# Conv and attention hybrid: the softmax division moved to GpSimd, the row maximum written negated, the score scale put into the query weights

## The chip, the core and the metric

The kernel runs on one core of a Trainium2 chip. The core has five engines that run side by side and meet only at semaphores: TensorE (PE, matmuls and transposes, results go to PSUM), VectorE (DVE), ScalarE (ACT), GpSimd (POOL, which works on SBUF here) and SyncE (SP, which starts the DMAs). The metric is the device time of one execution in microseconds; lower is better.

## The reference

The input is four images of 16 x 16 positions with 192 channels. Two layers follow each other.

Layer 0 is a group norm, a convolution, four directional scans over 256 positions with 16 states for each of 96 channels, a norm, a gate, an output projection, and a residual. Layer 1 is, per image (256 tokens), a Performer attention with 12 heads, a residual, and then an attention in which only 6 of the 12 heads are kept, chosen by a router. The change lies in this last attention:

```python
logits = router_in @ Wr + br
_, top_idx = jax.lax.top_k(logits, K)            # K = 6 of 12 heads
...
q = proj(Wq, bq) * m                             # m keeps the chosen heads
k = proj(Wk, bk) * m
v = proj(Wv, bv) * m
scores = jnp.einsum('bhqd,bhkd->bhqk', q, k) / jnp.sqrt(jnp.float32(D))   # D = 16
probs = jax.nn.softmax(scores, axis=-1)
ctx = jnp.einsum('bhqk,bhkd->bhqd', probs, v)
```

Per image and chosen head the scores are 256 x 256, and the softmax runs along the last axis.

## The kernel before

Each engine has its own program, in the order in which its function issues instructions. The scans of layer 0 come first, as 96 slots (8 scans of 12 units). In a slot DVE runs one scan of 512 positions for 128 rows (line 965), GpSimd multiplies the states with c_rep (L542), and PE sums them (L1336). Other work of the layers is woven in beside the slots.

After the slots comes the list `rest`, made once by `side_work()`: pairs of a step's name and an image number. All engines walk this same list and issue what a step has for them. Images 0 and 1 overlap, then 1 and 2, then 2 and 3, so that two or three images are on their way at a time. The steps of an image's last attention are `wqk`, `wv` (weights of the chosen heads, by matmuls against a selection), `fq`, `fk`, `fv` (queries, keys, values), and then `s0 t0 s1 w0 t1 w1`, `fo` and `rn`. The step `s0` handles heads 0, 2 and 4, `s1` heads 1, 3 and 5; `t0`/`t1` and `w0`/`w1` go with them. In this text a **round** is three heads, so there are 8 rounds of 3 heads: 24 heads in all. What happens to a head in a round:

- `s`: PE writes the scores into one PSUM bank, [128, 2, 256] (query position, query half, key). DVE takes the maximum of each row from PSUM (`row_max`, L1068), waits for it, and makes the bias -max/4 in a second small instruction (L1073). ACT computes exp(score/4 + bias) for each query half into `prob` and adds the row up into `psum_row` (`exp_scores`, L727).
- `t`: DVE takes the reciprocal of the two sums (L1079), waits for it, and multiplies the two halves of `prob` by it (`divide_by_sum`, L1082). PE waits for both halves and transposes `prob` in 4 blocks (`turn_probs`, L1358). ACT copies the result from PSUM to `probT` (L590).
- `w`: PE multiplies the values with `probT` (`weigh_values`, L1369); DVE copies the sum (L1088).

Image parity p picks one of two sets of small buffers and of `prob`. In the trace the second set of `prob` and `probT` lies in a shared room and is named room_s; room_g holds `res` (among others), room_w the second `wsel`.

GpSimd has little in `rest`: one small power per norm (L486, the reciprocal root of the variance, for `yT`, `o`, `p`, `fo`), a gate product (`yn`, L556) and the last residual (`rn`, L559, 128 x 384). For `wqk`, ACT copies the weights of the chosen heads out of PSUM into `wsel`, in 6 copies (L590): four of them are for the queries, two for the keys.

## Time and profile before

| | us |
|---|---|
| median of 3 runs | 490.98 (490.72 to 491.32) |
| the profiled execution, own time | 493.81 |
| its span, first to last instruction | 491.9 |
| PE busy | 357.9 (73%) |
| DVE busy | 371.5 (76%) |
| ACT busy | 182.3 (37%) |
| POOL busy | 199.2 (41%) |
| mean granted TensorE clock | 0.889 |

A group row of the profile names a line, engine, operation and tiles with their shapes, the number of instructions, the time they were busy and the mean duration of one, and what the engine waited for before them. An idle gap costs nothing if the engine is not the one that the end waits for; the chain of waits tells which one that is. The granted clock is a share of 2.4 GHz.

### The profile page before, as it was taken

The page shows a single profiled execution, that of the slowest core. Times are in us where ns is not written, and L with a number is a line of the kernel's source. Part 1 is how long each engine was busy: PE and PEld are TensorE (multiplying, and loading weights), DVE is VectorE, ACT ScalarE, POOL GpSimd, SP SyncE. Part 2 cuts the span into 40 slices and gives each one's busy share as a digit, 9 for nine tenths or more (in the row PEclk, how much of TensorE's full clock was granted, in tenths as well). Part 3 has the DMA queues.
Part 4 walks back from the last instruction along what each step waited for, and adds up shares of the span by engine and source line. Part 5 has one row for each costly group of instructions (what it writes and reads, how often), then busy time and mean ns, then how long its engine had stood idle before and what let it go on. Part 6 is the DMA issues. An engine that isn't in the chain of part 4 may idle for free. (4 is left out here: it accounts for less than half of the span.)

```text
span 491.9 us, 5371 instructions
## 1 busy us (share of the span) xinstructions
PE 357.9 (73%) x1545; PEld 205.6 (42%) x1545; DVE 371.5 (76%) x712; ACT 182.3 (37%) x442; POOL 199.2 (41%) x199
## 2 busy tenths in 40 slices
PE   5530575669678785765999998994787999967652
PEld 4310121214223321221647545543665485956441
DVE  6264599999899999999988999987556637255562
ACT  2235354325555462342333332335224401125541
POOL 4406375756678585774554553450020001000001
PEclk9999979777999797996999999898598989596867
DMA  6402221110111112101101000000000000000000
GB/s 130 83 0 63 48 47 27 43 36 13 33 44 38 38 39 53 33 19 40 33 9 45 24 16 0 1 0 2 0 18 0 2 0 17 0 1 1 2 16 16
DMA packets 15741, 12.66 MB, mean 26 GB/s; under 512 B 7279, under 2 KB 11361, under 8 KB 15713
## 3 DMA queue, kind: packets, MB, share of 16 engines
q1 hardware_dynamic: 15713, 12.33, 10.9%
q8 instruction: 12, 0.20, 0.2%
q14 instruction: 16, 0.13, 0.1%
HBM read 2.62 MB, written 0.79 MB: 7 GB/s over the span
## 5 line engine op out<-in xcount | busy, mean ns | idle before, releaser
L542 POOL TENSOR_TENSOR outp<-state,c_rep 128x512 f32<-128x512 f32 x96 | 129.1, 1350 | 95.4 <-DVE state L965 47.9
L965 DVE TENSOR_TENSOR_SCAN state<-decay,inp_bc 128x512 f32<-128x512 f32 x96 | 117.2, 1221 | 6.7 <-DVE inp_bc L956 3.2
L1336 PE MATMUL y_acc<-outp,band 128*96 128x512 f32 x192 | 109.7, 657 | 6.7 <-DVE y_sum L980 3.2
L704 ACT ACTIVATE decay<-step_bc,a_neg 128x510 f32<-128x510 f32 x96 | 64.9, 684 | 55.5 <-PE step_bc L1323 55.3
L956 DVE TENSOR_TENSOR inp_bc<-b_rep,inp_bc 128x512 f32<-128x512 f32 x96 | 65.5, 682 | 9.9 <-PE inp_bc L1327 9.8
L1327 PE MATMUL inp_bc<-room_s,spread 96*128 96x512 bf16 x96 | 41.0, 427 | 42.8 <-DVE state L965 42.4
L486 POOL TENSOR_TENSOR rs<-mv,neg_half 128x2 f32<-128x2 f32 x16 | 11.2, 698 | 132.4 <-DVE mv L1001 132.4
L1323 PE MATMUL step_bc<-room_s,spread 96*128 96x512 bf16 x96 | 40.5, 422 | 17.4 <-DMA room_s<-lo 14.3
L1327 PEld LDWEIGHTS inp_bc<-room_s,spread 96*128 96x128 bf16 x96 | 9.8, 102 | 83.4 <-DVE state L965 79.3
L1336 PEld LDWEIGHTS y_acc<-outp,band 128*96 128x96 f32 x192 | 34.1, 182 | 23.0 <-issue 10.2
L1323 PEld LDWEIGHTS step_bc<-room_s,spread 96*128 96x128 bf16 x96 | 10.4, 108 | 37.7 <-issue 29.0
L692 ACT CAST hi<-step 96x512 bf16<-96x512 f32 x16 | 9.9, 616 | 35.8 <-DVE step L935 27.2
L1428 PE MATMUL ring<-kvw,tT 96*128 96x480 f32 (+1 forms) x48 | 22.1, 585 | 0.0
L532 POOL TENSOR_TENSOR lo<-step,mid 96x512 bf16<-96x512 f32 x16 | 19.4, 1232 | 3.4 <-ACT mid L696 3.4
L1422 PE MATMUL ring<-tT,qw 96*128 96x256 f32 (+1 forms) x64 | 15.3, 381 | 0.8 <-issue 0.8
L1313 PE MATMUL ring<-room_g,pre_w 96*128 96x512 f32 x16 | 10.1, 719 | 7.5 <-DVE room_g L890 7.5
L884 DVE SCALAR_TENSOR_TENSOR room_e<-room_w,cw,room_e 96x544 f32<-96x544 f32 x16 | 15.1, 947 | 0.5
L525 POOL TENSOR_SCALAR sps<-spe 96x512 f32<-96x512 f32 x8 | 4.9, 618 | 23.6 <-ACT spe L683 23.6
L696 ACT CAST mid<-step 96x512 bf16<-96x512 f32 x16 | 9.9, 616 | 12.3 <-DVE step L948 12.0
L1422 PEld LDWEIGHTS ring<-tT,qw 96*128 96x128 f32 (+1 forms) x64 | 11.9, 189 | 5.3 <-issue 4.0
L1428 PEld LDWEIGHTS ring<-kvw,tT 96*128 96x128 f32 (+1 forms) x48 | 9.2, 198 | 10.0 <-issue 10.0
L527 POOL TENSOR_TENSOR sps<-sps,spe 96x512 f32<-96x512 f32 x8 | 12.8, 1599 | 0.7
(392 smaller groups left out, 665.1 us busy)
## 6 DMA issues: line engine op xcount, KB each, us to landing
b_rep<-bc SPq DMA_DIRECT2D x64, 32.0 KB, 2.0
c_rep<-bc SPq DMA_DIRECT2D x64, 32.0 KB, 2.0
room_s<-hi SPq DMA_DIRECT2D x24, 64.0 KB, 2.0
room_s<-mid SPq DMA_DIRECT2D x24, 64.0 KB, 2.0
room_s<-lo SPq DMA_DIRECT2D x24, 64.0 KB, 2.0
x_tok<-in_x_dram SPq DMA_DIRECT2D x2, 384.0 KB, 3.8
out_dram<-room_g SPq DMA_DIRECT2D x4, 192.0 KB, 2.0
room_a<-in_L_attn_w_qkv_dram SPq DMA_DIRECT2D x1, 432.0 KB, 6.4
```

The lines of the kernel that those rows point to most:

```text
L527: g.tensor_tensor(sps[:], sps[:], spe[:], ALU.mult).then_inc(S["sp_s"], 1)
L532: g.tensor_tensor(lo[:, i, :], step2[:, i, :], mid[:, i, :], ALU.subtract).then_inc(S["lo"], 1)
L542: g.tensor_tensor(outp[:, u % SLOTS, :], state[:, u % STATE_SLOTS, :], c_rep[:, n % 2, :], ALU.mult).then_inc(S["outp"], 1)
L704: a.activation(decay[:, u % SLOTS, :, 1:L], step_bc[u % 2][:, :].rearrange("p (b l) -> p b l", b=IMG)[:, :, 1:L], ACT.Exp, scale=a_neg[:, ...
L884: v.scalar_tensor_tensor(sums, window, cw[:, i:i + 1], sums, ALU.mult, ALU.add).then_inc(S["conv"], 1)
L956: v.tensor_tensor(inp_bc[u % 2][:, :], b_rep[:, n % 2, :], inp_bc[u % 2][:, :], ALU.mult).then_inc(S["drive"], 1)
L965: v.tensor_tensor_scan(state[:, u % STATE_SLOTS, :], decay[:, u % SLOTS, :, :].rearrange("p b l -> p (b l)"), inp_bc[u % 2][:, :], 0.0, AL ...
L1323: t_.matmul(step_bc[u % 2][:, :], spread[:, q, :], stack[:, n % 2, j, 0:TOK], start=True, stop=True).then_inc(S["bc_step"], 1)
L1327: t_.matmul(inp_bc[u % 2][:, :], spread[:, q, :], stack[:, n % 2, j, TOK:2 * TOK], start=True, stop=True).then_inc(S["bc_inp"], 1)
L1336: t_.matmul(y_acc[0:DI, :], band[:, at:at + DI], outp[:, u % SLOTS, :], start=(g12 == 0), stop=(g12 == UNITS - 1)).then_inc(S["y_mm"], 1)
L1422: ins = t_.matmul(b_[:, u * L:(u + 1) * L], qw[0:CK + c, c, i * P:(i + 1) * P], tT[0:CK + c, c, at0:at0 + L], start=(c == 0), stop=(c == 1))
L1428: ins = t_.matmul(b_[:, 0:w], tT[0:CK + c, c, at:at + P], kvw[0:CK + c, c, j, :], start=(c == 0), stop=(c == 1))
```

## The change

Three edits belong together. (1) The row maximum is written negated by the reduction itself, and the second small instruction (L1073), its buffer and its semaphore go. (2) The factor 1/4 leaves the exponential and is applied where ACT copies the selected query weights out of PSUM: four of the six copies become an activation (Copy) with a scale. (3) DVE keeps the reciprocal, and the two products by it move to GpSimd, into the same steps `t0` and `t1` of its list. DVE's reciprocal gets a wait for the division that last used its buffer.

```diff
--- before.py
+++ after.py
@@ -332,7 +332,6 @@
         col = sb("col", [CK, 3, 2, IMG])
         hot = sb("hot", [CK, 2, 2, IMG, TOPK])
         nmax = [sb(f"nmax{i}", [P, PER_ROUND, 2]) for i in range(2)]
-        nmaxs = [sb(f"nmaxs{i}", [P, PER_ROUND, 2]) for i in range(2)]
         psum_row = [sb(f"psum_row{i}", [P, PER_ROUND, 2]) for i in range(2)]
         prec = [sb(f"prec{i}", [P, PER_ROUND, 2]) for i in range(2)]
 
@@ -349,7 +348,7 @@
         S["outd"] = [sem(f"s_outd{b}") for b in range(IMG)]
         S["x"] = [sem(f"s_x{h}") for h in range(HALVES)]
 
-        for n in ("key", "prob_max", "prob_bias", "prob", "prob_rec", "prob_divided", "weighed"):
+        for n in ("key", "prob_max", "prob", "prob_rec", "prob_divided", "weighed"):
             S[n] = [sem(f"s_{n}{i}") for i in range(2)]
         free = [sem(f"s_free{i}") for i in range(FINAL_RING)]
         beside, rest = side_work()
@@ -542,6 +541,14 @@
                 g.tensor_tensor(outp[:, u % SLOTS, :], state[:, u % STATE_SLOTS, :], c_rep[:, n % 2, :],
                                 ALU.mult).then_inc(S["outp"], 1)
 
+            def divide_by_sum(n, j):
+                p = n % IMG
+                _, i, count = round_of(n, j)
+                pool.wait_ge(S["prob_rec"][p], count + 1)
+                for q in range(2):
+                    g.tensor_scalar(prob[p][:, i, q, :], prob[p][:, i, q, :], prec[p][:, i, q:q + 1], None,
+                                    ALU.mult).then_inc(S["prob_divided"][p], 1)
+
             def side(step, n):
                 h, b = n // IMG, n % IMG
                 ts = slice(2 * b, 2 * b + 2)
@@ -554,6 +561,9 @@
 
                     pool.wait_ge(S["norm_y"], 3 * (n + 1))
                     g.tensor_tensor(yn[:, ts, :], yn[:, ts, :], z[:, h, ts, :], ALU.mult).then_inc(S["gate"], 1)
+                if step in ("t0", "t1"):
+                    for j in range(int(step[1]), TOPK, 2):
+                        divide_by_sum(n, j)
                 if step == "rn":
                     pool.wait_ge(S["norm_r"], 4 * (n + 1))
                     g.tensor_tensor(res[:, ts, :], res[:, ts, :], x_tok[:, 2 * n:2 * n + 2, :], ALU.add).then_inc(S["fin"], 1)
@@ -719,13 +729,13 @@
                 p = n % IMG
                 _, i, count = round_of(n, j)
                 name = f"s{n}{j}"
-                act.wait_ge(S["prob_bias"][p], count + 1)
+                act.wait_ge(S["prob_max"][p], count + 1)
                 before = round_before(n, j)
                 if before:
                     fetched(act, "pt%d%d" % before)
                 for q in range(2):
                     a.activation(prob[p][:, i, q, :], bank(name)[:, q * L:(q + 1) * L], ACT.Exp,
-                                 bias=nmaxs[p][:, i, q:q + 1], scale=HD ** -0.5,
+                                 bias=nmax[p][:, i, q:q + 1],
                                  accum_out=psum_row[p][:, i, q:q + 1]).then_inc(S["prob"][p] if q == 0 else freed(name), 1)
 
             def side(step, n):
@@ -768,9 +778,11 @@
                     act.wait_ge(S["wsel_zero"], IMG)
                     src = bank(name)[:, 0:4 * CK].rearrange("p (i c k) -> p i c k", i=2, c=2)
                     heads = lambda ap, e: ap.rearrange("p (j e d) -> p j e d", e=2, d=HD)[:, :, e, :]
-                    evac(name, *[(heads(wsel[p][0:CK + c, c, e, :], e), heads(src[0:CK + c, 0, c, :], e))
-                                 for c in range(2) for e in range(2)],
-                         *[(wsel[p][0:CK + c, c, 2, :], src[0:CK + c, 1, c, :]) for c in range(2)])
+                    fetched(act, name)
+                    for c in range(2):
+                        for e in range(2):
+                            a.activation(heads(wsel[p][0:CK + c, c, e, :], e), heads(src[0:CK + c, 0, c, :], e), ACT.Copy, scale=HD ** -0.5)
+                    evac(name, *[(wsel[p][0:CK + c, c, 2, :], src[0:CK + c, 1, c, :]) for c in range(2)])
                 elif step == "wv":
                     src = bank(name)
                     if n == 0:
@@ -1065,23 +1077,20 @@
                 _, i, count = round_of(n, j)
                 name = f"s{n}{j}"
                 fetched(dve, name)
-                v.tensor_reduce(nmax[p][:, i, :], bank(name)[:, :].rearrange("p (q k) -> p q k", q=2), AX_X, ALU.max).then_inc(S["prob_max"][p], 1)
-                dve.wait_ge(S["prob_max"][p], count + 1)
                 before = round_before(n, j)
                 if before:
                     taken(dve, "s%d%d" % before)
-                v.tensor_scalar(nmaxs[p][:, i, :], nmax[p][:, i, :], -(HD ** -0.5), None, ALU.mult).then_inc(S["prob_bias"][p], 1)
-
-            def divide_by_sum(n, j):
+                v.tensor_reduce(nmax[p][:, i, :], bank(name)[:, :].rearrange("p (q k) -> p q k", q=2), AX_X, ALU.max,
+                                negate=True).then_inc(S["prob_max"][p], 1)
+
+            def invert_sum(n, j):
                 p = n % IMG
                 _, i, count = round_of(n, j)
                 taken(dve, f"s{n}{j}")
+                before = round_before(n, j)
+                if before:
+                    dve.wait_ge(S["prob_divided"][p], 2 * (round_of(*before)[2] + 1))
                 v.reciprocal(prec[p][:, i, :], psum_row[p][:, i, :]).then_inc(S["prob_rec"][p], 1)
-                dve.wait_ge(S["prob_rec"][p], count + 1)
-                for q in range(2):
-                    v.tensor_scalar(prob[p][:, i, q, :], prob[p][:, i, q, :], prec[p][:, i, q:q + 1], None,
-                                    ALU.mult).then_inc(S["prob_divided"][p], 1)
-
             def keep_heads(n):
 
                 dve.wait_ge(S["weighed"][n % IMG], n // IMG + 1)
@@ -1161,7 +1170,7 @@
                         row_max(n, j)
                 elif step in ("t0", "t1"):
                     for j in range(int(step[1]), TOPK, 2):
-                        divide_by_sum(n, j)
+                        invert_sum(n, j)
                 elif step == "w1":
                     keep_heads(n)
                 elif step == "fo":
```

The two places in the order of instructions, before and after. On VectorE, image 3, from the last two row maxima of step `s0` over step `rn` of image 2 to the first division of `t0` (inp_bc1 and y_acc are PSUM banks); before:

```order
L1068 TENSOR_REDUCE nmax1<-inp_bc1 128x2
L1073 TENSOR_SCALAR nmaxs1<-nmax1 128x2
L1068 TENSOR_REDUCE nmax1<-y_acc 128x2
L1073 TENSOR_SCALAR nmaxs1<-nmax1 128x2
L1018 SCALAR_TENSOR_TENSOR room_g<-room_g,mv,gb 128x192 x2
L1024 SCALAR_TENSOR_TENSOR room_g<-room_g,rs,gb 128x192 x2
L1079 RECIPROCAL prec1<-psum_row1 128x2
L1082 TENSOR_SCALAR room_s<-room_s,prec1 128x256 x2
```

The same place after, up to the first maximum of `s1`:

```order
L1083 TENSOR_REDUCE nmax1<-inp_bc1 128x2
L1083 TENSOR_REDUCE nmax1<-y_acc 128x2
L1030 SCALAR_TENSOR_TENSOR room_g<-room_g,mv,gb 128x192 x2
L1036 SCALAR_TENSOR_TENSOR room_g<-room_g,rs,gb 128x192 x2
L1093 RECIPROCAL prec1<-psum_row1 128x2 x3
L1083 TENSOR_REDUCE nmax1<-step_bc0 128x2
```

The small instructions between the maxima are gone, and three reciprocals stand in a row where reciprocal and products took turns. On GpSimd, the end of the list, from the residual of image 0 or 1 on; before:

```order
L559 TENSOR_TENSOR room_g<-room_g,x_tok 128x384
L486 TENSOR_TENSOR rs<-mv,neg_half 128x2 x3
L559 TENSOR_TENSOR room_g<-room_g,x_tok 128x384
L486 TENSOR_TENSOR rs<-mv,neg_half 128x2
L559 TENSOR_TENSOR room_g<-room_g,x_tok 128x384
```

And after:

```order
L569 TENSOR_TENSOR room_g<-room_g,x_tok 128x384
L485 TENSOR_TENSOR rs<-mv,neg_half 128x2 x2
L549 TENSOR_SCALAR prob<-prob,prec 128x256 x12
L485 TENSOR_TENSOR rs<-mv,neg_half 128x2
L569 TENSOR_TENSOR room_g<-room_g,x_tok 128x384
L549 TENSOR_SCALAR room_s<-room_s,prec 128x256 x12
L485 TENSOR_TENSOR rs<-mv,neg_half 128x2
L569 TENSOR_TENSOR room_g<-room_g,x_tok 128x384
```

The divisions of image 2 (x12: two rounds) now stand between the powers of the norms, and those of image 3 behind the residual of image 2.

## Rows read from the trace of the kernel before

**Rows 1.** Busy time by stretch: start:end, length, busy us (instructions), clock, DMA, GB/s.
```profile
34.00:318.00 284.00, 211.51 (x709) 95.84 (x710) 257.18 (x352) 117.03 (x220) 169.11 (x140) 0.91 0.14 32
325.00:492.00 167.00, 124.79 (x751) 94.73 (x749) 92.36 (x310) 53.43 (x196) 16.44 (x20) 0.82 0.02 6
```

**Rows 2.** Groups of DVE instructions from 320 to 492, by shape.
```profile
L1082 DVE TENSOR_SCALAR prob<-prob,prec 128x256 f32<-128x256 f32 x24 | 7.4, 351 | 0.4
L1073 DVE TENSOR_SCALAR nmaxs<-nmax 128x2 f32<-128x2 f32 x24 | 4.7, 196 | 0.8
L1079 DVE RECIPROCAL prec<-psum_row 128x2 f32<-128x2 f32 x24 | 3.8, 158 | 0.0
```

**Rows 3.** Timeline, DVE: start us, us, engine, line, operation, names, shapes.
```profile
340.43 0.68 DVE L1068 TENSOR_REDUCE nmax<-inp_bc 128x2 f32<-128x512 f32 x1
...
341.23 0.69 DVE L1068 TENSOR_REDUCE nmax<-y_acc 128x2 f32<-128x512 f32 x1
...
373.21 0.69 DVE L1115 TENSOR_SCALAR room_b<-inp_bc 128x512 f32<-128x512 f32 x1
373.81 0.16 DVE L1079 RECIPROCAL prec<-psum_row 128x2 f32<-128x2 f32 x1
```

**Rows 4.** Chain of waits, pieces in order of time: start, us, what.
```profile
334.30 0.62 DVE prob L1082 x2
...
335.06 2.79 PE ring L1358 x12
...
349.29 0.63 DVE prob L1082 x2
...
350.05 1.09 PE step_bc L1358 x4
...
456.56 0.44 PE y_acc L1358 x4
...
468.37 1.39 DVE room_s L1082 x2
...
469.89 2.79 PE ring L1358 x12
...
477.24 0.63 DVE room_s L1082 x2
...
478.00 1.09 PE y_acc L1358 x4
```

**Rows 5.** Groups of POOL instructions over the whole span, by shape.
```profile
L525 POOL TENSOR_SCALAR sps<-spe 96x512 f32<-96x512 f32 x8 | 4.9, 618 | 23.6 <-ACT spe L683 23.6
L559 POOL TENSOR_TENSOR room_g<-room_g,x_tok 128x384 f32<-128x384 f32 x4 | 4.0, 994 | 12.0 <-DVE room_g L1024 12.0
...
L556 POOL TENSOR_TENSOR room_f<-room_f,z 128x192 f32<-128x192 f32 x4 | 2.4, 590 | 11.0 <-DVE room_f L1024 11.0
...
L482 POOL MEMSET room_w<- 96x648 f32 x1 | 0.6, 637 | 0.0
...
L455 POOL MEMSET room_b<- 96x384 f32 x1 | 0.4, 416 | 0.0
```

**Rows 6.** Timeline: a small DVE instruction beside GpSimd's, and GpSimd's residual.
```profile
328.53 2.49 POOL L542 TENSOR_TENSOR outp<-state,c_rep 128x512 f32<-128x512 f32 x2
...
330.25 0.79 DVE L1073 TENSOR_SCALAR nmaxs<-nmax 128x2 f32<-128x2 f32 x1
...
468.33 0.99 POOL L559 TENSOR_TENSOR room_g<-room_g,x_tok 128x384 f32<-128x384 f32 x1 [3.14 <-DVE room_g L1024]
```

**Rows 7.** Timeline, PE and DVE, where something else bounds a round.
```profile
328.34 3.83 PE L1336 MATMUL y_acc<-outp,band 128*96 128x512 f32 x8
...
387.61 1.35 PE L1358 MATMUL step_bc<-ident,room_s 128*128 128x128 f32 x8 [1.03 <-DVE room_s L1082]
...
441.22 2.05 PE L1476 MATMUL step_bc<-ident,valr 1*96 1x1 f32 x12 [2.19 <-DVE valr L1061]
```

**Rows 8.** Timeline, ACT: an activation (Copy) and a plain copy of one shape.
```profile
338.78 0.37 ACT L750 ACTIVATE tT<-step_bc 96x256 f32<-96x256 f32 x1
...
363.35 0.37 ACT L590 COPY fk<-inp_bc 96x256 f32<-96x256 f32 x1 [0.23 <-PE inp_bc L1500]
```

## The prediction, made before the changed kernel ran

> **What bounds the kernel now.** I read the busy time by stretch first. Up to 318 us the scans keep DVE busy 257.2 of 284 us [rows 1]; the change touches nothing there but ACT's copies of one image's weights. All 24 heads of the softmax lie behind 325 us, where of 167 us PE is busy 124.8, DVE 92.4 and POOL 16.4 [rows 1]. PE is the busiest there, but it is not alone on the path: the chain of waits goes back and forth, DVE dividing, PE transposing [rows 4]. In seven of the eight rounds PE stands still until DVE's first division is done (334, 349, 374, 387, 445, 468 and 477 us; four of them stand in [rows 4]). The eighth is hidden: at 456.56 PE comes to its transposes straight from other matmuls [rows 4]. After each round's third division DVE waits for PE, so DVE's own time behind a division is worth nothing. What counts is when the first division ends, and whether the next two come as fast as PE transposes: 2.79 us for three heads, 0.93 each [rows 4], about 0.88 inside the other groups, but 0.68 at full clock (1.35 for two) [rows 7].
>
> **The small instruction that goes (edit 1).** 24 x 196 ns = 4.7 us of DVE [rows 2]. The step matters more than the duration: from one maximum to the next takes 0.80 us (340.43 to 341.23) for a reduction of 0.68, since the small instruction waits for it. An instruction that reads as much from PSUM with nothing waiting for it lets the next begin after 0.60 (373.21 to 373.81) [rows 3]. A negated maximum is not in the trace; I price it as the plain one. So a head saves 0.20 - 0.01 = 0.19 us and a round 0.57, on DVE. ACT's first exponential also starts 0.2 us earlier. If the reductions follow only at their full 0.69, a head saves 0.1 and a round 0.3; that is the lower bound of this gain.
>
> **The division on GpSimd (edit 3).** DVE: 0.351 us for each half [rows 2], 0.62 for the pair [rows 4]. GpSimd has no product by a per-row scalar in the trace. From below: half of the 96x512 TENSOR_SCALAR, 618/2 = 309 ns [rows 5]. From above: a product of two tensors goes at (994 - 590)/192 = 2.1 ns an element, so 590 + 64 x 2.1 = 0.72 us for 256 [rows 5]. The nearest row is the TENSOR_SCALAR. An element of one-stream work costs (637 - 416)/264 = 0.84 ns (two memsets) [rows 5], so 256 fewer cost 618 - 215 = 0.40 us. I take 0.40, the pair 0.76 with a small overlap, and 0.04 us more for the signal between engines. The first division of a round then ends about 0.2 us later after its reciprocal than now. The three come 0.76 apart against 0.72 on DVE, still under PE's 0.88.
>
> The Trainium skill ("GPSIMD Engine Reference", section "4.1 Engine selection") speaks against moving elementwise work here: two inputs are about twice as slow as on VectorE, one input is about line rate. The trace bears the first half out, 590 ns for 192 elements of a two-tensor product [rows 5]; whether a scalar per row counts as a second input is what the 0.40 and the 0.72 stand for.
>
> **The exponent's scale (edit 2).** 16 of 24 copies of selected weights become activations. An ACT activation Copy of 96x256 takes 0.37 us, a plain copy of that shape 0.37 [rows 8]; priced at nothing. These copies lie ahead of PE's query matmuls and cover each other. If the activation took 0.05 more, 4 x 0.05 = 0.2 us would stand in front of `fq` for an image, mostly while PE does other steps.
>
> **The added waits.** DVE's reciprocal waits for the division that used its buffer a round or two images before, long done: nothing. POOL now waits in its queue for reciprocals; behind them stand the norms' powers, which come from later DVE instructions in the same list, so nobody waits longer, save for one place: image 3's first division stands behind the residual L559. That residual already holds the division back now: DVE's first pair takes 1.39 us instead of 0.62 [rows 4], beside L559 from 468.33 to 469.32 [rows 6].
>
> **Round by round** (gain negative, us at the first transposes). Each starts with -0.57 +0.20 = -0.37 where all three maxima lie on DVE's path just ahead of the division.
> - 334: the sum of the scans' output waits for PE until 328.34 + 3.83 = 332.17 [rows 7], so of the saving about 0.3 is left: -0.1.
> - 349: -0.37. 374: the same; the third head then comes 0.3 earlier: -0.35.
> - 387: the maxima are not ahead of it (DVE waits for a key matmul): +0.2, and PE is at full clock with 0.68 a head, so GpSimd's 0.76 shows: +0.26.
> - 445: DVE waits for PE's column products until 441.22 + 2.05 = 443.27 [rows 7], now 443.38: -0.1 + 0.2 = +0.1.
> - 456: hidden, 0.
> - 468: L559 starts 0.57 earlier, ends 468.75; division to 469.48, PE at 469.62 instead of 469.89: -0.27.
> - 477: the sums of the first head are there 0.2 earlier and the maxima end 0.4 to 0.6 earlier; reciprocal 476.45, division 476.69 to 477.45, PE 477.6 instead of 478.0: -0.4.
>
> Sum: -0.1 - 0.37 - 0.35 + 0.26 + 0.1 + 0 - 0.27 - 0.4 = -1.13 us. Against the profiled execution: 493.81 - 1.1 = 492.7 us, span 490.8. That is 0.23%; the same share of the median 490.98 gives 489.8 us.
>
> **Rivals.**
> (A) *GpSimd's scalar product costs as much as a product of two tensors*, 0.72 us, pair about 1.38. For it: it must fetch a value per row, and no row shows the form. Against it: the only TENSOR_SCALAR runs at 1.2 ns an element. Then the first division of seven rounds ends 0.6 us later still, +4.3, and a head comes every 1.38 instead of 0.88: two heads in six rounds, +6.0, less what round 374 and 477 wait for anyway: together about +9, 499.5 us. It decides from about 0.5 us for one instruction: there the first divisions have cost 7 x 0.2 = 1.4 more and the gain is gone.
> (B) *One instruction at 0.45 to 0.6 us*: between no change and +3, 490 to 494 us.
> (C) *The gain of the maxima is real and GpSimd takes 0.31 to 0.35*: 7 x 0.1 to 0.2 better, -1.9 to -2.4, 488.8 us.
> (D) *DVE and GpSimd hold each other up.* For it: a small DVE instruction took 0.79 us instead of 0.17 beside a GpSimd product [rows 6], and the division waited for L559. The reciprocals of heads 2 and 3 could be held by GpSimd's first pair, and each pair would start only after 0.16 + 0.08 more: 1.0 a head against 0.88, +0.25 in six rounds and +0.6 at 387: +2.1, 491.9 us. Against it: in most rounds all sums are ready, and the three reciprocals go out before GpSimd starts. The Trainium skill ("SBUF — State Buffer", section "Who interferes with whom") says that whichever of the two starts first keeps the shared port pair for the whole instruction. By that, the removal of 48 DVE products leaves fewer instructions that need it, and its cost would be that of (D).
> (E) *The change does nothing that counts*: PE's own work after each round sets the end (PE is busy 75% of this stretch), and what is won before one product is lost at the next wait for another image: within 0.5 us.
>
> **Chances.** Forecast with (C), GpSimd at most 0.45 and the gain kept: 0.45 (0.35 and 0.10). (E) 0.17. (D) 0.10. (B) 0.16, half of it slower by more than 0.2%. (A) 0.12. A measurement of this kernel can tell 0.2%, about 1 us, from no change. Faster than 490.0: nearly all of the forecast with (C), 0.43. Slower than 492.0: (A) 0.12, half of (B) 0.08, half of (D) 0.05, 0.25. The rest, 0.32, is within. The likeliest time is 489.8. From below the range takes in (C) and a little more for gains that add up, 488.2; from above (D) and (B) to 494.0. It leaves out (A) and a few per cent on either side.
>
> **What would show it.** The GpSimd product group: mean near 400 ns if right, over 500 if (A) or (B). The step between two maxima: 0.60 us. PE's gap from the end of the reciprocal to the first transpose: 0.98 us instead of 0.79 (334.27 to 335.06). The transposes of a round still 2.6 to 2.8 us for three heads; stretched to 3.5 and more by (A). The reciprocals at 158 ns each, three in a row; one at 0.5 or more would be (D). DVE busy less by 17 + 4.7 us, which by itself tells nothing of the time. The forecast is wrong if GpSimd's scalar product is slow, or if the chain after 325 us turns out to run through PE past the divisions.

## The result, and the profile of the changed kernel

The changed kernel takes 526.39 us (median of 4 runs, 525.06 to 530.17), the kernel before beside it 491.15 (4 runs, 490.72 to 492.56). The ratio is 1.0709 with a 95% interval of 1.0674 to 1.0743: 35 us slower, where 489.8 us in a range of 488.2 to 494.0 was forecast. The profiled execution took 525.06 us, with a span of 523.3. (Ratios here and below are made from undisturbed executions alone, two of them for e6, so a ratio can differ a little from that of the two medians, and since the profiles of e1, e9, e10 and e15 fell in disturbed executions, only single instructions, paces and waits are read from them.)

The page of the changed kernel: busy time, then the chain that ended last, as shares of the span by engine and by line.

```profile
PE 382.9 (73%) x1545; PEld 214.7 (41%) x1545; DVE 349.5 (67%) x640; ACT 182.8 (35%) x442; POOL 242.8 (46%) x247
...
PE 25%; POOL 9%; DVE 7%; issue 2%; ACT 0%; POOLq 0%; DVEq 0%; ACTq 0%
POOL prob L549 4%; POOL room_s L549 4%; PE y_acc L1345 2%; DVE nmax L1083 1%; PE ring L1492 1%; PE ring L1445 1%; PE y_acc L1455 1%; PE ring L1431 1%; PE ring L1367 1%; PE inp_bc L1437 1%; PE ring L1437 1%; PE ring L1524 1%; PE ring L1378 1%; PE ring L1499 1%; DVE hot L1158 1%
```

The chain is the path of work and waits, followed back from the last instruction; POOLq, DVEq and ACTq are the queues of the engines, and "issue" is time with no wait that the profile shows. Its first two lines are now the division on GpSimd, L549: 8% of the span. The stretches of [rows 1], in the changed kernel: start:end, length, busy us (instructions) of PE, PEld, DVE, ACT and POOL, granted clock, DMA share, GB/s.

```profile
34.00:318.00 284.00, 219.61 (x723) 99.27 (x722) 256.73 (x354) 118.52 (x221) 170.47 (x142) 0.85 0.14 32
325.00:523.00 198.00, 141.95 (x728) 101.21 (x726) 69.70 (x230) 52.91 (x195) 57.94 (x66) 0.70 0.02 5
```

Up to 318 us DVE is as busy as before (257.18 and 256.73 of 284 us), and the change has next to nothing there. Still the two traces differ: PE's clock is 0.91 in one and 0.85 in the other, and the last scan starts at 328.41 us before and at 324.67 in the changed kernel. That is a difference between executions and not the change's: `e3_immediate` and `e8_product_and_add` below, which are the changed kernel but for GpSimd's products, start it at 327.02 and 324.66. A tail cut at 325 us therefore grows only from 167 to 198 us; from the start of the last scan to the end it is 163.5 us before and 198.6 now, 35 us more, the whole loss. Behind 325 us DVE has 22.7 us less to do and that brings nothing. GpSimd has 41.5 us more, and PE's clock fell from 0.82 to 0.70 of full speed. This fall is not of the kind seen ahead of 318 us: the trace of e3, whose products are nearly as slow, has 0.90 up to 318 us, close to the kernel before, and 0.69 from 325 us on. The rows that answer to [rows 5], groups of POOL instructions from 318 us on, by shape (busy us, mean ns, then idle us before and its releaser):

```profile
L549 POOL TENSOR_SCALAR prob<-prob,prec 128x256 f32<-128x256 f32 x24 | 21.7, 926 | 23.9 <-DVE prec L1093 23.9
L549 POOL TENSOR_SCALAR room_s<-room_s,prec 128x256 f32<-128x256 f32 x24 | 21.7, 925 | 11.1 <-DVE prec L1093 11.1
```

One product takes 926 ns, where 400 were forecast and 720 was the upper bound. What that does in a round, in the timeline of the first one (start us, us, engine, line, operation, names, shapes, and in brackets the wait before and its releaser):

```profile
325.81 1.86 DVE L1083 TENSOR_REDUCE nmax<-ring 128x2 f32<-128x512 f32 x3
...
330.02 0.28 DVE L1093 RECIPROCAL prec<-psum_row 128x2 f32<-128x2 f32 x3
330.28 5.44 POOL L549 TENSOR_SCALAR prob<-prob,prec 128x256 f32<-128x256 f32 x6 [3.02 <-DVE prec L1093]
...
332.27 1.08 PE L1367 MATMUL ring<-ident,prob 128*128 128x128 f32 x4 [3.85 <-POOL prob L549]
...
334.07 1.09 PE L1367 MATMUL ring<-ident,prob 128*128 128x128 f32 x4 [0.72 <-POOL prob L549]
...
335.87 1.09 PE L1367 MATMUL ring<-ident,prob 128*128 128x128 f32 x4 [0.71 <-POOL prob L549]
```

Three maxima take 1.86 us, so each begins 0.59 us after the one before it: the 0.60 of the forecast. The three reciprocals are through within 0.28 us. Then six products need 5.44 us, 1.81 a head against 0.72 on DVE. PE gets a head every 1.80 us instead of every 0.93. From the first reciprocal to the end of the last transposes it is 330.02 to 336.96, 6.9 us. Before, the reciprocal began at 334.11 and the transposes ended at 335.06 + 2.79 = 337.85 [rows 4]: 3.7 us. That is 3.2 us more for this round. Counted in the same way, six of the seven rounds in which PE waits grew by 3.2 to 3.3 us and that of 387 by 3.9: 23 us in all. Also, four transposes last 1.09 us here, and 0.66 where PE is at 2.4 GHz.

The chain of waits of the changed kernel, four of its eight rounds (start, us, what):

```profile
330.28 5.45 POOL prob L549 x6
335.87 1.09 PE ring L1367 x4
...
397.53 5.44 POOL room_s L549 x6
403.11 1.09 PE inp_bc L1367 x4
...
476.32 5.43 POOL prob L549 x6
...
504.00 5.43 POOL room_s L549 x6
509.57 1.10 PE ring L1367 x4
```

All eight rounds stand in the chain (the others at 349.01, 381.00, 462.98 and 493.27), that of 476.32 too: it is the round of 456.56 in [rows 4], which DVE's division did not bound. That it stands there with 5.43 us does not mean that it costs 5.43. PE goes into it from other matmuls at 480.58 without a wait, and waits only for the third head, 0.28 us at 481.89; till then its own work is a path almost as long.

The second loss is PE's clock. Three stretches of PE work, first of the kernel before, then the same work in the changed one (columns as above):

```profile
352.10:359.50 7.40, 6.29 (x49) 5.39 (x48) 2.58 (x9) 1.93 (x8) 0.69 (x1) 0.81 0.00 0
...
359.50:369.00 9.50, 8.69 (x47) 6.87 (x45) 4.53 (x16) 2.54 (x10) 2.39 (x3) 1.00 0.08 23
...
399.10:437.90 38.80, 36.21 (x202) 30.08 (x200) 17.39 (x59) 6.99 (x31) 3.09 (x4) 0.82 0.02 5
```

```profile
354.60:364.70 10.10, 9.57 (x49) 7.67 (x50) 2.68 (x9) 1.36 (x7) 0.72 (x1) 0.50 0.00 0
...
364.70:376.50 11.80, 10.99 (x47) 8.40 (x45) 4.53 (x16) 2.54 (x10) 2.39 (x3) 0.80 0.06 19
...
416.40:455.50 39.10, 36.52 (x201) 30.41 (x199) 17.43 (x59) 7.00 (x31) 3.11 (x4) 0.82 0.02 6
```

The first stretch lies right behind a round's waits. Before, it ran at a mean of 0.81; now it runs at 0.50 throughout, the lower of the clock's two levels (1.2 GHz), and takes 10.1 us instead of 7.4. The second took 9.5 us at full clock and now takes 11.8 at 0.80, with the same 47 matmuls. The third, further behind its last wait, is as it was. So in this pair of traces the clock takes its share in the stretches right behind the rounds.

### The profile page after: what moved, and what is told of

It reads as the page before. It is cut to its first block and busy times, and to the rows that moved or that the text cites. A ratio compares the mean times of both kernels' runs of the same rounds, so it can differ in the third digit from the quotient of the medians.

```text
span 523.3 us, 5365 instructions
## 1 busy us (share of the span) xinstructions
PE 382.9 (73%) x1545; PEld 214.7 (41%) x1545; DVE 349.5 (67%) x640; ACT 182.8 (35%) x442; POOL 242.8 (46%) x247
## 5 line engine op out<-in xcount | busy, mean ns | idle before, releaser
L1345 PE MATMUL y_acc<-outp,band 128*96 128x512 f32 x192 | 112.9, 675 | 7.2 <-DVE y_sum L992 3.2
L549 POOL TENSOR_SCALAR prob<-prob,prec 128x256 f32<-128x256 f32 x24 | 21.7, 926 | 23.9 <-DVE prec L1093 23.9
L549 POOL TENSOR_SCALAR room_s<-room_s,prec 128x256 f32<-128x256 f32 x24 | 21.7, 925 | 11.1 <-DVE prec L1093 11.1
L1431 PE MATMUL ring<-tT,qw 96*128 96x256 f32 (+1 forms) x64 | 16.7, 406 | 0.8 <-issue 0.8
L1367 PE MATMUL ring<-ident,room_s 128*128 128x128 f32 x28 | 7.6, 428 | 11.3 <-POOL room_s L549 11.3
```

The costliest lines, as they stand in the source:

```text
L549: g.tensor_scalar(prob[p][:, i, q, :], prob[p][:, i, q, :], prec[p][:, i, q:q + 1], None, ALU.mult).then_inc(S["prob_divided"][p], 1)
L1345: t_.matmul(y_acc[0:DI, :], band[:, at:at + DI], outp[:, u % SLOTS, :], start=(g12 == 0), stop=(g12 == UNITS - 1)).then_inc(S["y_mm"], 1)
L1431: ins = t_.matmul(b_[:, u * L:(u + 1) * L], qw[0:CK + c, c, i * P:(i + 1) * P], tT[0:CK + c, c, at0:at0 + L], start=(c == 0), stop=(c == 1))
```

## The experiments

The diffs are against the changed kernel unless it is said otherwise. Line numbers in the rows are those of each kernel.

**Which edit is it?** `e1_dve_divides` keeps edits 1 and 2 and gives the products back to DVE.

```
-                if step in ("t0", "t1"):
...
-                        divide_by_sum(n, j)
...
                 v.reciprocal(prec[p][:, i, :], psum_row[p][:, i, :]).then_inc(S["prob_rec"][p], 1)
+                dve.wait_ge(S["prob_rec"][p], count + 1)
+                for q in range(2):
+                    v.tensor_scalar(prob[p][:, i, q, :], prob[p][:, i, q, :], prec[p][:, i, q:q + 1], None,
+                                    ALU.mult).then_inc(S["prob_divided"][p], 1)
```

> The changed kernel with the two products of a head put back on DVE, behind the reciprocal: the negated maximum and the moved scale stay. Theory: the loss is GpSimd's product alone and the other edits gain what they were priced at. A maximum follows the one before after 0.60 us instead of 0.80; the seven rounds that PE waits for save 0.3 + 0.57 + 0.5 + 0 + 0.1 + 0.57 + 0.5 = 2.5 us, so 488.6 us. Rival: the gain is swallowed by PE's own chain: 490.5 to 491.5 us. Rival: an edit other than the product costs as well: over 492 us.

Measured: 490.0 us, ratio 0.996 (0.9923 to 0.9998). Its maxima in the timeline:

```profile
329.35 1.86 DVE L1080 TENSOR_REDUCE nmax<-ring 128x2 f32<-128x512 f32 x3
```

The pace of 0.59 us is there, and edits 1 and 2 together bring about 0.4%, 2.0 us; the interval allows anything from 0.1 to 3.8 us. `e2_division_alone` is the counterpart: the kernel before, with its scaled maxima and its copies, and only the division on GpSimd.

> The kernel before with nothing but the division moved to GpSimd: the small instruction behind each maximum and the scale in the exponential stay. Theory: the cost is all from this edit and adds to the others' gain: the changed kernel's ratio 1.071 over 0.996 is 1.075, 528 to 530 us. Rival: the edits interact (the division hides the gain, since the first division waits for GpSimd anyway): the same 1.071 as the changed kernel, 526 us or less.

Measured: 529.1 us, 1.073 (1.0701 to 1.0758). 0.996 x 1.073 = 1.0687, against 1.0709: the edits add up within the intervals, and the loss is the division's.

**Why is the product slow?** Three kernels change only the instruction in `divide_by_sum`. `e3_immediate` multiplies by a constant (the division by the sums is left out). `e4_broadcast_product` multiplies two tensors, the second being the reciprocal repeated 256 times. `e8_product_and_add` gives the same instruction a second operation, an added zero.

```
-    g.tensor_scalar(prob.., prob.., prec[p][:, i, q:q + 1], None, ALU.mult)
e3+  g.tensor_scalar(prob.., prob.., 0.00390625, None, ALU.mult)
e4+  g.tensor_tensor(prob.., prob.., prec[p][:, i, q:q + 1].to_broadcast([P, L]), ALU.mult)
e8+  g.tensor_scalar(prob.., prob.., prec[p][:, i, q:q + 1], 0.0, ALU.mult, ALU.add)
```

> The changed kernel with GpSimd's product by the constant 1/256 instead of the reciprocal of the row's sum; the division is left out, all waits stay. Theory: it is the factor per row that makes the instruction 0.926 us long. With a constant it takes 0.40 us, as the 96x512 TENSOR_SCALAR (618 ns) less 256 elements, and the whole kernel takes the 489.8 us that the sum gave for this price. Rival: a 128x256 product in place takes 0.9 us whatever the factor: 526 us. Rival: the instruction is short but the hand-over to another engine costs in its own right: 493 to 500 us.

> The changed kernel with GpSimd's product written as a product of two tensors, the second being the reciprocal repeated along the row. Theory: 0.72 us an instruction, the line through 590 ns for 192 and 994 ns for 384 elements, so a round of six takes 4.3 instead of 5.44 us; eight rounds save 9 us and some clock: 512 to 517 us. Rival: the repeated operand is no cheaper than the per-row factor, 0.9 us: 526 us.

> The changed kernel with a second operation in GpSimd's product: times the reciprocal of the row, plus 0.0; the result is the same. So far: the form with one operation takes 926 ns with a factor per row and 852 ns with a constant for 256 elements, but the scan's TENSOR_SCALAR with two constants and two operations takes 618 ns for 512. Theory: the form without a second operation is the slow one. Then this takes about 0.4 to 0.5 us, the round 2.7 us, and the kernel 489 to 492 us. Rival: what differs is something else (in place, 128 rows instead of 96, the factor per row): it stays at 0.9 us and the time at 526 us.

Measured: 524.3 us, 1.0664 (1.0637 to 1.0691) for e3; 502.79, 1.0241 (1.019 to 1.0293) for e4; 501.94, 1.0187 (1.0151 to 1.0223) for e8. The POOL groups of e3, e4 and e8, in this order:

```profile
L549 POOL TENSOR_SCALAR prob<-prob 128x256 f32<-128x256 f32 x24 | 19.7, 852 | 24.1 <-DVE prec L1093 24.1
```

```profile
L549 POOL TENSOR_TENSOR prob<-prob,prec 128x256 f32<-128x256 f32 x24 | 13.9, 614 | 22.1 <-DVE prec L1093 22.1
```

```profile
L549 POOL TENSOR_SCALAR prob<-prob,prec 128x256 f32<-128x256 f32 x24 | 11.0, 479 | 22.1 <-DVE prec L1093 22.1
```

The expectations of e3 (its theory), e4 and e8 were missed in part. The constant did not bring 0.40 us. e4's product took 0.614 us instead of 0.72, and the kernel 9 us less than the 512 at the least. e8's product came out at the 0.4 to 0.5 us expected, but its kernel 10 us above the 489 to 492.

The value per row is not what costs: with a constant the product still takes 852 ns. What costs is the form with one operation. The same product with a second, empty operation takes 479 ns, about half of 926, and even a product of two tensors is quicker than the plain one. `e5_half_the_columns` (one run; half of the columns stay undivided) measures how the plain form grows:

```
-                    g.tensor_scalar(prob[p][:, i, q, :], prob[p][:, i, q, :], ...
+                    g.tensor_scalar(prob[p][:, i, q, 0:P], prob[p][:, i, q, 0:P], ...
```

> The changed kernel with GpSimd's product over the first 128 columns of 256; half of the division is left out. Theory: a cost per element of about (926 - 100)/256 = 3.2 ns, so 0.51 us an instruction, a round of 3.0 us, the kernel 493 to 498 us. Rival: a fixed cost of some 0.7 us for each instruction: still 0.8 us or more, the kernel at 515 us or more.

```profile
L549 POOL TENSOR_SCALAR prob<-prob,prec 128x128 f32<-128x128 f32 x24 | 14.0, 603 | 22.3 <-DVE prec L1093 22.3
```

Both expectations were too low: 603 ns, and 505.03 us. (926 - 603)/128 = 2.5 ns an element, and 0.28 us beside it, if the two points lie on a line.

**Is it only the division's duration?** With e8's 479 ns, close to the 0.40 forecast, the kernel is still 1.9% slower, where the prediction drew the line of no gain at 0.5 us. `e6_pe_kept_busy` leaves the changed kernel's division alone and gives PE idle transposes of the identity to do ahead of each wait, 12 before a round's first head and 4 before the others (they write a bank that the real transposes then overwrite):

```
                     b_ = begin(f"pt{n}{j}")
+                    for _ in range(12 if j == r else 4):
+                        t_.transpose(b_[:, 0:P], idn, idn)
                     pe.wait_ge(S["prob_divided"][p], 2 * (round_of(n, j)[2] + 1))
```

> The changed kernel with idle transposes on PE in front of its wait for a division: 12 before the first head of a round, 4 before each of the others, written to the bank that the head's own transposes then fill. The 0.907 us pace of GpSimd explains 8 x 3.1 = 25 us of a span longer by 31.4. Theory: the other 6 to 9 us come from PE running at its lower clock after the long waits (mean granted clock behind 325 us 0.70 against 0.82, PE busy 142 against 125 us with the same instructions). With the idle transposes the clock stays up and the time falls by 4 to 9 us, to 517 to 522 us. Rival: the clock is not what the waits cost: 526 us or more, as the added instructions only delay.

Measured: 507.5 and 508.5 us, 1.0326 (1.0296 to 1.0357): twice the gain of 9 us that was expected at most. First the tail of the changed kernel, then e6's tail and its first round:

```profile
318.00:523.00 205.00, 148.09 (x763) 105.00 (x761) 75.10 (x240) 54.79 (x201) 61.33 (x69) 0.71 0.01 5
```

```profile
318.00:507.00 189.00, 144.97 (x929) 110.97 (x927) 76.32 (x242) 55.83 (x203) 62.16 (x70) 0.88 0.02 5
...
331.18 1.53 PE L1365 MATMUL ring<-ident 128*128 128x128 f32 x12 [1.16 <-DVE y_sum L1002]
...
333.78 0.66 PE L1369 MATMUL ring<-ident,prob 128*128 128x128 f32 x4 [1.07 <-POOL prob L549]
```

With 160 transposes more (the rows count 166, as some records are missing from a trace), the tail is 16 us shorter: the clock granted is 0.88 instead of 0.71, and four transposes take 0.66 us instead of 1.08. Up to 318 us both traces have a clock of 0.85. The heads still come 1.80 us apart, so the division is as slow as it was. The same was then done with the better kernels, 8 idle transposes ahead of the first head in seven of the eight rounds: `e7_dve_divides_pe_busy` (on e1), `e9_before_pe_busy` (on the kernel before), `e10_product_and_add_pe_busy` (on e8).

```
+                    for _ in range((8 if j == r else 0) if (n, r) not in ((2, 1),) else 0):
+                        t_.transpose(b_[:, 0:P], idn, idn)
```

> Negated maximum and moved scale, division on DVE, and 8 idle transposes on PE ahead of the wait for a round's first division, in the seven rounds in which PE waits. Theory (the lower clock after a wait costs this kernel too): the transposes run in the wait, the clock stays at its higher level behind it, and behind 325 us the mean clock rises from about 0.82 to 0.9 or more: 484 to 488 us. Rival: the waits of the kernel before are too short to matter, or the 8 transposes reach into the division's end: 489 to 491 us.

> The kernel before with nothing changed but 8 idle transposes on PE ahead of a round's first division, in seven rounds. Theory: the gain of the clock (1.3% over the kernel with edits 1 and 2) stands by itself and adds to their 0.4%: ratio 0.986 to 0.990, 484.5 to 486.5 us. Rival: the transposes only help since the other edits shorten the waits: 490 us or more.

> GpSimd's product with the second operation (0.48 us) and 8 idle transposes on PE ahead of a round's first division, in seven rounds. The open point: with that product GpSimd's round takes 2.75 us, near VectorE's, and the rounds themselves came out within tenths of the kernel before, yet the kernel took 502 us; the trace puts the loss into stretches with no division in them, 358 to 370 and 389 to 446 us of its span, at a clock of 0.81 and 0.76. Theory: these are the lower clock that follows PE's slightly longer waits. With the transposes these stretches run at 1.00 and 0.8 again, and the time is that of the kernel with the division on VectorE and the same transposes, plus 0.2 us a round and a little pace: 485 to 488 us. Rival: GpSimd's work costs in another way: 495 us or more.

Measured: e7 484.47 us, 0.9835 (0.9809 to 0.9861); e9 488.18, 0.9889 (0.9854 to 0.9924); e10 496.41, 1.0015 (0.9972 to 1.0059). e7 is quicker than both kernels. e10 missed its 485 to 488 us; its ten executions took 489.55 to 499.85, nearer to the rival's 495 or more. It gains 1.7% over e8, but stays 1.8%, some 9 us, behind e7. First rounds of e7 and of e10:

```profile
333.04 0.66 PE L1369 MATMUL ring<-ident,prob 128*128 128x128 f32 x4 [0.21 <-DVE prob L1091]
...
333.86 1.35 PE L1369 MATMUL ring<-ident,prob 128*128 128x128 f32 x8 [0.16 <-DVE prob L1091]
```

```profile
331.97 0.66 PE L1369 MATMUL ring<-ident,prob 128*128 128x128 f32 x4 [0.60 <-POOL prob L549]
332.98 0.63 PE L1369 MATMUL ring<-ident,prob 128*128 128x128 f32 x4 [0.35 <-POOL prob L549]
```

At full clock PE does a head in 0.66 us, and DVE's 0.72 keeps up almost; GpSimd's 0.92 lets it wait before every head of this round. From the first reciprocal to the last transposes the seven rounds are 0.4 to 1.2 us longer in e10 than in e7, 5.1 us together. That is somewhat more than half of the 9 us; the rest is not explained.

`e11_more_idle_transposes` adds to e7 28 idle transposes in place of 8 ahead of the longest wait and 16 ahead of two column products:

```
+                    for _ in range(16 if n in (0, 3) else 0):
+                        t_.transpose(b_[:, 0:P], idn, idn)
                     pe.wait_ge(S["val_rows"], n + 1)
```

> Division on VectorE, negated maximum, moved scale, and more idle transposes: 28 instead of 8 in the longest wait (image 3, first round, 4.5 us), and 16 ahead of the router's column products of images 0 and 3 (4.0 and 2.2 us of wait). Theory: stretches behind these waits, at a clock of 0.77 in the kernel with 8, come up to 0.85 or more: ratio 0.975 to 0.980 to before. Rival: the rest of the lower clock comes from elsewhere (long busy stretches lose it too, 0.82 in the attention of images 2 and 3): 0.983 as with 8, or worse where the transposes reach past the wait.

Measured: 483.5 us, 0.981 (0.9751 to 0.9868), between the two expectations and not clearly better than e7.

**Is GpSimd itself the cause, or the time?** e8 left two readings: the time to the first head and between heads, or something about GpSimd and DVE working side by side. Four kernels take e1 and delay DVE's division with additional DVE instructions; GpSimd does nothing there. `e12_dve_slower_division` adds one small instruction a head:

```
                 dve.wait_ge(S["prob_rec"][p], count + 1)
+                v.tensor_scalar(outp[:, 0, 0:184], band[:, 0:184], 1.0, None, ALU.mult)
```

> Division on VectorE, negated maximum, moved scale, no idle transposes, and one more VectorE instruction ahead of each head's two products: 128x184, result unused, about 0.19 us. So a round on VectorE has the pace of GpSimd's product with the second operation: 0.92 us a head instead of 0.72, the first division 0.2 us later. Theory: it is the time of the division alone, with the clock that follows from PE's waits, that costs; who does it is all one. Then the kernel takes what that one took, 499 to 502 us (ratio 1.015 to 1.022). Rival: 0.2 us later and 0.2 a head slower cost only what they add up to, 2 to 3 us over the 490 of the kernel without them, 492 to 493 us (ratio 1.000 to 1.004), and GpSimd's part in the loss is another.

Measured: 491.27 us, 0.9973 (0.9952 to 0.9994) at 0.89 us a head. That is not e8's 1.0187, and for the moment spoke for the second reading. `e14_dve_same_waits` then came closer to e8's waits (400 columns ahead of a round's first head, 190 ahead of the others):

```
+                w = 400 if j < 2 else 190
+                v.tensor_scalar(outp[:, 0, 0:w], state[:, 0, 0:w], 1.0, None, ALU.mult)
```

> As the kernel with the 128x184 instruction, but 128x400 ahead of the first head of a round and 128x190 ahead of the others, so that PE's wait for the first division has the length that it has with GpSimd's product and add (2.9, 2.3, 2.3, 1.4, 3.2 us), which is 0.2 to 0.35 longer than it was. Theory: those tenths decide in which level the clock is for the dense stretches behind the rounds: 497 to 502 us. Rival: they cost 7 x 0.25 = 1.8 us and no more: 492 to 494 us, and the other 8 us of GpSimd's kernel come with GpSimd.

Measured: 1.0094 (1.0069 to 1.012), 496.49 us, at 0.90 us a head, which lies between the two expectations. One round and the dense stretch behind it, first in e12, then in e14:

```profile
383.66 0.63 PE L1368 MATMUL step_bc<-ident,room_s 128*128 128x128 f32 x4 [1.19 <-DVE room_s L1092]
...
395.40:434.10 38.70, 36.12 (x201) 30.51 (x200) 17.32 (x59) 6.99 (x31) 3.08 (x4) 0.82 0.02 6
```

```profile
382.46 0.63 PE L1369 MATMUL step_bc<-ident,room_s 128*128 128x128 f32 x4 [1.30 <-DVE room_s L1093]
...
395.10:439.60 44.50, 41.91 (x201) 35.36 (x199) 17.44 (x59) 6.89 (x31) 3.08 (x4) 0.71 0.02 5
```

The first waits of the seven rounds are 0.11 to 0.19 us longer in e14, and 201 matmuls take 44.5 us at a mean of 0.71 instead of 38.7 at 0.82. In e8, whose first waits are 0.10 to 0.16 us longer again, the same stretch takes 42.0 at 0.76:

```profile
403.60:445.60 42.00, 39.41 (x201) 33.24 (x199) 17.43 (x59) 6.98 (x31) 3.08 (x4) 0.76 0.02 6
```

It is the stretch that in the changed kernel, with waits longer by about another us, ran at 0.82 (416.40 to 455.50). So the clock behind a wait does not follow the wait in proportion, and a few us of the difference between two kernels hang on it. That tenths of a microsecond in the waits are what moves it is likely but not shown: these are single traces, and their clocks differ up to 318 us as well (0.89 in e12, 0.85 in e14, 0.84 in e8), where the kernels do the same. To be clear of it, the last two go to large delays. `e13_dve_at_gpsimd_pace` adds one 128x1024 instruction, and `e15_dve_at_full_pace` three, so that DVE's division is as slow as GpSimd's:

```
e13, e15 +   v.tensor_scalar(outp[:, 0:2, :], state[:, 0:2, :], 1.0, None, ALU.mult)
e15 +        v.tensor_scalar(outp[:, 2, :], state[:, 2, :], 1.0, None, ALU.mult)
e15 +        v.tensor_scalar(decay.., state.., 1.0, None, ALU.mult)   (512 columns for the first head, 256 for the others)
```

> Division on VectorE, negated maximum, moved scale, and one more VectorE instruction ahead of each head's two products: 128x1024, result unused, 1.07 us. A head then takes 1.79 us on VectorE, the pace that GpSimd's products of 0.926 us have in the changed kernel (1.81). Theory: what the changed kernel loses is the time of the division and the clock that goes with PE's waits, whoever does it: 520 to 527 us, ratio 1.058 to 1.071, mean clock behind 318 us about 0.70. Rival: GpSimd costs in a way of its own (the kernel with GpSimd at 0.48 us was 2% slower than this one with a similar pace on VectorE): 510 to 516 us.

> Division on VectorE, negated maximum, moved scale, and three more VectorE instructions ahead of each head's two products (results unused): 128x1024 (0.61 us of pace in the last kernel of this kind, which made 1.33 us a head), 128x512 and 128x256, 128x512 for a round's first head. A head then takes 1.8 us and the first division ends 2.0 to 2.2 us after its reciprocal, the changed kernel's times, with GpSimd out of it. Theory: it is the time of the division and PE's clock behind it: 522 to 527 us, ratio 1.062 to 1.072. Rival: GpSimd brings a loss of its own of some 8 us (as the 479 ns product against VectorE at its pace): 514 to 519 us.

e13's additional instruction took 0.61 us of pace and not the 1.07 it was sized for, so a head comes every 1.33 us: 511.72 us, 1.0402 (1.037 to 1.0433). That lies in its rival's 510 to 516 us, but at this pace it tells nothing for the rival. e15: 526.69 us, 1.0689 (1.061 to 1.0767). Its first round:

```profile
333.03 1.09 PE L1370 MATMUL ring<-ident,prob 128*128 128x128 f32 x4 [3.83 <-DVE prob L1094]
...
334.89 1.09 PE L1370 MATMUL ring<-ident,prob 128*128 128x128 f32 x4 [0.78 <-DVE prob L1094]
...
336.76 1.09 PE L1370 MATMUL ring<-ident,prob 128*128 128x128 f32 x4 [0.78 <-DVE prob L1094]
```

With no product on GpSimd, with waits of 3.83 and 0.78 us (3.85 and 0.72 in the changed kernel) and a head every 1.86 us, the kernel takes what the changed one does, 1.0689 against 1.0709. The first waits of all seven rounds agree within 0.06 us. So the loss comes without GpSimd when the heads come as late. The interval of e15 leaves room for a part of GpSimd's own of up to about 1%, 5 us, not for the 8 us of the rival. The kernels in the order of their pace:

| kernel | us a head | ratio |
|---|---|---|
| e1, DVE divides | 0.72 | 0.996 |
| e12, DVE | 0.89 | 0.9973 |
| e14, DVE | 0.90, the first 0.1 later | 1.0094 |
| e8, GpSimd, two operations | 0.92 | 1.0187 |
| e4, GpSimd, two tensors | 1.16 | 1.0241 |
| e13, DVE | 1.33 | 1.0402 |
| changed kernel | 1.81 | 1.0709 |
| e15, DVE | 1.86 | 1.0689 |

## Why the prediction was wrong, point by point

**The step that failed first** is the term "I take 0.40" for GpSimd's product. It measured 0.926 us, above even the upper bound of 0.72. The nearest row was taken by the instruction's name, TENSOR_SCALAR, and scaled by its elements [rows 5]. But L525 is another form: it has two constant operations, a product and a sum. In that form the product here takes 0.479 us, which the scaled row, 0.40, nearly gave. The form with one operation was in no row, and neither bound held for it. Nor was the two-tensor product a ceiling. The question that the prediction asked, whether a value per row counts as a second input, was the wrong one: with a constant it is 0.852.

The Trainium skill ("GPSIMD Engine Reference", section "4.1 Engine selection") puts elementwise work with one input at roughly line rate. Only the form with two operations comes near that here (479 ns against DVE's 351 for the same tile [rows 2]; by pace 0.46 us against 0.27); the form with one takes 926. For the half on two inputs the prediction's row of 590 ns has no row of VectorE beside it; the page of the kernel before has 1350 ns for a product of two 128x512 tiles on GpSimd (L542) and 682 on DVE (L956).

**The second step that failed** has no line in the sum: the clock of PE. The transposes of a round were priced at the durations of before, and everything behind them at no change. Behind the longer waits PE ran at 1.2 GHz where it had been partly or wholly at 2.4. Rival (A) had the mechanism of the time right (first head late, PE fed at GpSimd's pace), and for 0.72 us a product it gave +9 us (on the forecast of 489.8 that is 498.8, not the 499.5 that stands there). e4 has 0.614 us a product and lost 2.4%, 12 us. For the same reason "about 0.5 us" as the point where it turns was wrong: at 0.479 the kernel is already 1.9% slower.

**How the 35 us divide.** Idle transposes bring the changed kernel from 1.0709 to 1.0326, 18.8 us, and the kernel before from 1 to 0.9889, 5.4 us. The difference, 13.4 us, is about what the change costs in clock. Between the two kernels with PE kept busy lie 1.0326 - 0.9889 = 0.0437, 21.4 us: about the time of the division itself. That the two add up to the loss follows from how they are made and checks nothing. The check is the count from rows: the seven rounds' 23 us, less the 2.0 that edits 1 and 2 bring, are 21. Both parts are estimates to some us: each ratio has an interval of 0.3%, e6 has more idle transposes than e9, and the rounds counted from rows hold some slower transposes.

**"456: hidden, 0"** nearly held, although the round now stands in the chain: PE waits 0.28 us in it. Even at 1.81 us a head the division there runs beside PE's other matmuls.

**What held.** The place: the first division's end and the pace of the heads are what counts, the chain after 325 us runs through the division. The maxima at 0.60 us (0.59). Edit 1 and 2 together, counted as 2.5 us (the sum of -1.1 and 7 x 0.2), brought 2.0. Edit 2 shows no cost. DVE's lower busy time told nothing of the kernel's time. (D) did not come about: the 24 reciprocals take 154 ns on average, 158 before [rows 2], and in the round shown all three are through within 0.28 us. That most of the loss is not in two engines holding each other up is what e15 shows.

**What stays open.** From e12 over e14 to e8 the first waits grow by 0.1 to 0.2 us at each step (2.72, 1.98, 2.04, 1.19 us at the first four rounds in e12; 2.83, 2.17, 2.15, 1.30 in e14; 2.94, 2.33, 2.25, 1.40 in e8), and the time by 1.2% and 0.9%, 4 to 6 us. Seven rounds with 0.1 to 0.2 us more are 1 us. The rest may be the clock, as the stretches above suggest, or for e8 a part of GpSimd's own. No run separates the two, nor does one explain the 4 us of e10 that its rounds leave over.

## What to carry to other kernels

Price an instruction by its exact form (number of operations, kind of factor, number of tensors), not by its name and its elements; where no row has that form, the nearest row is no bound, and a kernel with only that instruction changed tells it at once. An engine that PE waits for in a dependent chain costs twice, by its own time and by the clock PE has behind the wait: here an estimated 21 and 13 us. Idle transposes ahead of such waits brought more than they cost here, and with edits 1 and 2 they gave the best kernels of this study, 0.9835 and 0.981 of the time before.

## What the runs showed of the hardware

- On GpSimd, a TENSOR_SCALAR over 128x256 f32 takes 926 ns with one operation and a factor per row, 852 with one operation and a constant, and 479 with the factor per row and an added zero. A TENSOR_TENSOR with a repeated second operand takes 614. Why the form with one operation is the slow one, no run shows.
- On DVE, a product by a constant from SBUF to SBUF lets the next instruction start after 0.61 us for 1024 columns, 0.34 for 512 and 0.20 for 256, in e15's first round (330.99 to 331.60 to 331.94, and 333.94 to 334.14). The product in place by a value per row takes 0.27 for 256 columns: a pair takes 0.62 and one of them 0.351.
- PE's clock is worth several per cent in a kernel whose PE waits only some us at a time: keeping PE busy ahead of the waits took 3.8% off the changed kernel and 1.1% off the one before. The Trainium skill ("TensorE: Matmul & The Clock Gate", section "What's actually happening") puts the ramp penalty under 1% of a typical kernel's span. It says so of the slow matmuls at a kernel's start; in this kernel the clock falls again behind waits in the middle, and by the runs above that costs more.
